# Cross-attention over 128-wide heads: the TensorE order of a two-head turn and its PSUM banks

## The chip, the core and the metric

The kernel runs on one core of a Trainium2 chip. A core has TensorE (matrix products into PSUM, 8 banks of 128x512 fp32), VectorE (DVE), ScalarE (ACT), GpSimd (POOL) and SyncE (SP, which here issues the DMAs). Each engine works through its own queue in order and waits on semaphores for the others. The metric is the device time of one execution in microseconds.

## The reference, cut to what matters

Four transformer blocks run one after the other on x (8, 128, 256). The change is in the third, which is two cross-attentions of 16 heads of width 128 against the same context (8, 128, 256):

```
for i in (1, 2):
    h = layer_norm(x, scale_i, offset_i)
    qh = (h @ wq + bq).reshape(b, 128, 16, 128)
    kh = (ctx @ wk + bk).reshape(b, 128, 16, 128)
    vh = (ctx @ wv + bv).reshape(b, 128, 16, 128)
    kh = concatenate([kh, bias_k]); vh = concatenate([vh, bias_v])   # one more key and value
    weights = softmax(einsum('bqhk,bthk->bhqt', qh, kh) / sqrt(128))
    x = x + einsum('bhqt,bthk->bqhk', weights, vh).reshape(b, 128, 2048) @ wo + bo
```

All is fp32. The kernel subtracts bias_k and bias_v from keys and values beforehand, so that the extra key is a score of zero and bias_v is added back to every head's output.

## The kernel before

It has three stages: stage A (the first two blocks), the two cross-attentions (`TURNS`), and stage C (an MLP and the fourth block). Stages A and C follow orders written out by hand in tables (`ORDER_ONE`, `ORDER_TWO`); the change does not touch them. `TURNS` is a loop over (j, turn): j = 1 or 2 is the attention, turn = 0 to 7 a pair of heads. Every engine has its own copy of this loop, and the order of the calls in each copy is the order of its queue. In a turn TensorE makes, for its two heads h = 0, 1:

- Q and K (`project_heads`, L830): a head's queries or keys for all 8 batches, two banks, 12 products of 128x512 each (every fp32 operand is cut into a high and a low part, and three of the four part products are made);
- V (`values_of`, L844): values of both heads for two batches, four calls of 12 products, a bank each;
- S (`scores_of`, L858): 16 matmuls, two banks; T (`turn_weights`, L867): 8 transposes of the softmax weights, two banks; W (`weigh_heads`, L878): weights times values, 16 matmuls, two banks;
- O (`output`, L890): the projection of the turn before, four calls of 12 products, a bank each.

`claim` makes the first write of a bank wait until the bank's last contents are drained. VectorE drains S (maximum L1195 and shift L1200; the bank is free after the shift), V (L1220), Q (L971) and O (L1239, into x), makes the sums and reciprocals (L1207, L1211) and the low part of the heads' outputs (`OT lo`, L1227). ScalarE makes the exponentials, drains K (L1343) and T (L1510, into `PT`), and makes the high part of the heads' outputs (L1343). GpSimd divides by the sum (L1742), cuts the weights of later heads into parts (L1701, L1703) and copies two bias columns per head into `bcol` and a pair per turn into `bvcol` (L1732, L1733, L1792), from which the drains read them. SyncE loads the weights.

Banks before: S of head 0 in banks 0, 1 and of head 1 in 2, 3; T of both heads in 4, 5; W in 6, 7 (head 0 of turn 0: 2, 3); Q and K by `BANKS`. In turn 0 three of the four V calls are made ahead in banks 2, 3, 4 (`AHEAD`), and the fourth (called V3 below) goes to bank 5. TensorE's order in an ordinary turn is S0, O, O, Q1, K1, O, O, S1, V, V, V, V, T0, Q0', W0, T1, K0', W1, where the digit is the head and ' marks the next turn. Turn 0 is Q1, S0, S1, V3, Q0', K0', T0, T1, W0, W1. In the last turn K0' is replaced by other work (in j = 1 the first keys of j = 2, in j = 2 keys and values of stage C).

## Time and profile before

| | |
|---|---|
| median of 3 runs | 1048.21 us (1047.02 to 1049.92) |
| profiled execution, span | 1047.5 us |
| median less the profiled span | 0.7 us |
| stage A | 0 to about 299 us |
| turns of j = 1 and j = 2 | about 299 to 798 us |
| stage C | from about 798 us |
| an ordinary turn | 31.37 us, TensorE busy throughout |
| TensorE / VectorE / ScalarE / GpSimd busy | 97% / 68% / 57% / 59% |

The trace is of one execution. Its times run from the start of the span. A row of the timeline gives an instruction's start and duration; TensorE's matmuls overlap, so that what a block of them costs is the distance from its start to the start of the next block. The chain of waits follows the work that ended last back through what released it.

### The profile page before, as it was taken

Reading aid. Unit: us, or ns where it says so; the run is one execution under the profiler, and the core shown is the slowest. Engines: PE = TensorE matmul, PEld = TensorE weight load, DVE = VectorE, ACT = ScalarE, POOL = GpSimd, SP = SyncE. Lnnn points to the kernel's source line nnn. Section 1 sums busy time; section 2 is a strip of 40 time slices with the busy share of each in tenths; the row PEclk is TensorE's granted clock in tenths of the full one; section 3 lists DMA queues with packets and bytes.
Section 4 is the critical chain, followed back from the end, with each engine's and each line's share of the span. In section 5 each row is a group of like instructions: output and inputs, shape, how many; then the busy total and the mean of one; then the engine's idle time right before and its main releaser. Section 6 shows DMA issues by size and latency. Waiting matters only on the chain.

```text
span 1047.5 us, 21298 instructions
## 1 busy us (share of the span) xinstructions
PE 1011.3 (97%) x8275; PEld 908.5 (87%) x8275; DVE 711.9 (68%) x1141; ACT 593.4 (57%) x1296; POOL 614.3 (59%) x617
## 2 busy tenths in 40 slices
PE   7899999999999999999999999999998999989998
PEld 6788888888888999999988999999998888777877
DVE  7997888998266565655567655656556287898760
ACT  5998888797533333222334323332225479999982
POOL 5895476655554443333376445655444388999961
PEclk9999999999999999999999999999999999999999
DMA  9200001000112221202130111101000000000000
GB/s 340 103 2 2 1 2 42 2 1 2 51 61 81 81 82 61 78 25 81 41 104 1 42 40 42 41 21 41 22 10 2 1 1 2 2 1 2 12 12 21
DMA packets 33788, 40.74 MB, mean 39 GB/s; under 512 B 2111, under 2 KB 31257, under 8 KB 32025
## 3 DMA queue, kind: packets, MB, share of 16 engines
q1 hardware_dynamic: 33689, 39.38, 11.3%
q8 instruction: 67, 1.10, 0.4%
q14 instruction: 32, 0.26, 0.1%
HBM read 38.32 MB, written 1.05 MB: 38 GB/s over the span
## 4 chain that ended last, share of the span: by engine, by line
PE 73%; POOL 11%; DVE 6%; issue 5%; ACT 5%; DMA 0%; SPq 0%; POOLq 0%; DVEq 0%; ACTq 0%
PE psum L830 13%; PE psum L715 9%; PE psum L727 9%; PE psum L890 7%; PE psum L844 7%; PE psum L753 5%; PE psum L878 5%; PE psum L858 4%; POOL C tile L1647 3%; PE psum L642 3%; PE psum L743 3%; PE psum L768 2%; PE psum L867 2%; POOL C tile L1653 2%; PE psum L780 1%
## 5 line engine op out<-in xcount | busy, mean ns | idle before, releaser
L1742 POOL TENSOR_TENSOR B tile<-B tile,B rec 128x1024 f32<-128x1024 f32 x32 | 60.7, 1897 | 192.0 <-DVE B rec L1211 192.0
L1653 POOL TENSOR_TENSOR A tile<-A tile,outer rec 128x1024 f32<-128x1024 f32 x48 | 91.0, 1906 | 57.8 <-DVE outer rec L1089 57.7
L1428 ACT ACTIVATE A tile<-A tile,outer min 128x128 f32<-128x128 f32 (+1 forms) x256 | 92.3, 449 | 2.6 <-DVE outer min L1082 2.5
L1343 ACT ACTIVATE B kT<-psum,B bcol 128x1024 f32<-128x1024 f32 x32 | 35.7, 1115 | 98.9 <-PE psum L830 98.9
L1239 DVE TENSOR_TENSOR x_all<-x_all,psum 128x512 f32<-128x512 f32 x64 | 42.6, 683 | 55.2 <-PE psum L890 55.0
L1428 ACT ACTIVATE C tile<-C tile,outer min 128x128 f32<-128x128 f32 x256 | 77.8, 398 | 0.5 <-DVE outer min L1082 0.4
L1499 ACT ACTIVATE B tile<-B max 128x8 f32<-128x8 f32 x32 | 6.9, 215 | 123.4 <-DVE B max L1195 123.4
L971 DVE TENSOR_SCALAR B qT<-psum,B bcol 128x1024 f32<-128x1024 f32 x32 | 41.1, 1283 | 48.8 <-PE psum L830 48.7
L844 PE MATMUL psum<-B v hi,cT hi 128*128 128x256 f32 x256 | 73.5, 287 | 0.3 <-ACT B kT L1343 0.3
L844 PE MATMUL psum<-B v hi,cT lo 128*128 128x256 f32 x256 | 71.9, 281 | 0.0
L844 PE MATMUL psum<-B v lo,cT hi 128*128 128x256 f32 x256 | 71.9, 281 | 0.0
L878 PEld LDWEIGHTS psum<-B PT,B v 128*128 128x128 f32 x512 | 61.4, 191 | 3.4 <-ACT B PT L1510 1.4
L1653 POOL TENSOR_TENSOR C tile<-C tile,outer rec 128x1024 f32<-128x1024 f32 x32 | 60.6, 1898 | 6.0 <-DVE outer rec L1089 6.0
L878 PE MATMUL psum<-B PT,B v 128*128 128x128 f32 x512 | 62.1, 275 | 1.0 <-ACT B PT L1510 1.0
L1075 DVE TENSOR_TENSOR A tile<-m,psum 128x1024 f32<-128x1024 f32 x48 | 56.5, 1215 | 9.2 <-PE psum L743 8.0
L858 PE MATMUL psum<-B kT,B qT 128*128 128x128 f32 x512 | 62.1, 275 | 0.0
L1394 ACT COPY A PT<-psum 128x512 f32<-128x512 f32 x96 | 51.4, 591 | 18.1 <-PE psum L753 10.9
L1087 DVE TENSOR_REDUCE outer sum<-A tile 128x4 f32<-128x1024 f32 (+1 forms) x48 | 58.0, 1207 | 4.9 <-ACT A tile L1428 4.9
L858 PEld LDWEIGHTS psum<-B kT,B qT 128*128 128x128 f32 x512 | 59.9, 192 | 0.2
L1227 DVE SCALAR_TENSOR_TENSOR B OT1 lo<-psum,B bvcol,B OT1 hi 128x512 fp32r<-128x512 f32 x32 | 24.0, 751 | 51.3 <-ACT B OT1 hi L1343 50.1
L727 PE MATMUL psum<-weights,C aT 128*128 128x256 f32 x256 | 57.2, 380 | 1.2 <-ACT C aT L1385 1.2
L727 PE MATMUL psum<-weights,A aT 128*128 128x256 f32 x256 | 57.8, 380 | 0.1
(294 smaller groups left out, 3470.6 us busy)
## 6 DMA issues: line engine op xcount, KB each, us to landing
weights<-in_weights_c SPq DMA_DIRECT2D x6, 1024.0 KB, 6.3
raw<-in_wq SPq DMA_DIRECT2D x32, 128.0 KB, 2.6
raw<-in_wk SPq DMA_DIRECT2D x32, 128.0 KB, 2.9
raw<-in_wv SPq DMA_DIRECT2D x16, 256.0 KB, 2.8
raw<-in_wo SPq DMA_DIRECT2D x16, 256.0 KB, 2.7
weights<-in_weights_a SPq DMA_DIRECT2D x1, 3072.0 KB, 21.9
weights<-in_weights_a SPq DMA_DIRECT2D x1, 2048.0 KB, 11.3
wide<-in_bias_v SPq DMA_DIRECT2D x2, 1024.0 KB, 9.5
```

The lines of the kernel that those rows point to most:

```text
L715: i = pe.matmul(bank(z)[:, n * T:(n + 1) * T], w[wp][:, c, n * P:(n + 1) * P], h[hp][:, c, :], start=(c, wp, hp) == (0, 0, 0), stop=c == C ...
L727: i = pe.matmul(bank(z)[:, 0:D], part.aT(k)[:, c, b * P:(b + 1) * P], w2[:, c, :], start=c == 0, stop=c == FC - 1)
L830: i = pe.matmul(bank(banks[n]), wt[wp][:, c, :], src[sp][:, c, n * BANK:(n + 1) * BANK], start=(c, wp, sp) == (0, 0, 0), stop=c == C - 1 a ...
L844: i = pe.matmul(bank(z)[:, k * 2 * HK:(k + 1) * 2 * HK], m.bcT[cp][:, c, (2 * n + k) * S:(2 * n + k + 1) * S], m.cut["v"][wp][:, c, :], st ...
L858: i = pe.matmul(bank(2 * h + b // 4)[:, (b % 4) * S:(b % 4 + 1) * S], m.qT[h][:, b * S:(b + 1) * S], m.kT[h][:, b * S:(b + 1) * S], start= ...
L878: i = pe.matmul(bank(z)[:, k * P:(k + 1) * P], m.vv[:, 4 * n + k, h * HK:(h + 1) * HK], m.bPT[:, h, n, k * P:(k + 1) * P], start=True, sto ...
L890: i = pe.matmul(bank(z)[:, k * D:(k + 1) * D], m.bOT[h][op][:, (2 * n + k) * S:(2 * n + k + 1) * S], m.cut["o"][wp][:, h, :], start=(h, op ...
L1075: dve.tensor_tensor(tile(u, ly.nk), mask.to_broadcast(shape), sc, ALU.subtract).then_inc(s["masked"].sem, s["masked"].mark((st, u)))
L1087: dve.tensor_reduce(part.sum[:, u % 4, 0:ly.per], tile(u, ly.nk), AX.X, ALU.add).then_inc(s["sum_made"].sem, s["sum_made"].mark((st, u)))
L1428: i = act.activation(of_head, of_head, ACT.Exp, bias=part.min[:, u % 4, h:h + 1], scale=-1.0)
L1653: pool.tensor_tensor(tile(u, ly.nk), tile(u, ly.nk), part.rec[:, u % 4, 0:ly.per].unsqueeze(2).to_broadcast([P, ly.per, ly.nk]), ALU.mult) ...
L1742: pool.tensor_tensor(tv, tv, m.brec[:, h, :].unsqueeze(2).to_broadcast([P, B, S]), ALU.mult).then_inc(s["normalised"].sem, s["normalised"] ...
```

## The change

The loops are regrouped and the banks are dealt out anew.

- TensorE's ordinary turn becomes seven groups: S0 S1, O O O O, K0' K1', V V V V, T0 T1, Q0' Q1', W0 W1. Both heads of the next turn are projected in this turn. Turn 0 becomes Q1, S0, S1, V3, K0', K1', Q0', Q1', T0, T1, W0, W1, and the last turn has no Q' and, for K', the same other work as before, after T1.
- Banks alternate: an even turn's first set is banks 0 to 3 and its other set 4 to 7, in an odd turn the reverse. S, K', T and W use the first set; O, V and Q' use the other, which is the first set of the next turn. Turns 0 and 7 have exceptions. In turn 0, K0' goes to banks 4 and 5, K1' to 6 and 7, Q0' and Q1' to 0 to 3; V3 stays in bank 5.
- The queues of VectorE, ScalarE, GpSimd and SyncE are put in an order that goes with it: VectorE takes both heads' maxima and shifts first, ScalarE drains both K' before both T, GpSimd cuts weights in pairs and divides both heads one after the other, and SyncE loads weights in pairs.
- `bcol` and `bvcol`, their copies on GpSimd and the waits on them are gone. Drains read the bias column of a head in the table of columns (`cols`).

Nothing else is computed and the number and shapes of the matmuls are the same. The diff, cut to its core:

```diff
-BANKS = {("q", 0): (0, 1), ("k", 0): (2, 3), ("q", 1): (6, 7), ("k", 1): (4, 5)}
-def banks_of(kind, head):
-    return BANKS["q", 1] if (kind, head) == ("k", 2) else BANKS[kind, head % 2]
+def first_set(turn):
+    return turn % 2 * 4
+def other_set(turn):
+    return 4 - first_set(turn)
+FIRST_BANKS = {(1, "q", 0): 0, (1, "k", 0): 2, (1, "q", 1): 6, (1, "k", 1): 4, (2, "q", 0): 0, (2, "k", 0): 4, (2, "q", 1): 6, (2, "k", 1): 4}
+def head_bank(j, kind, head):
+    if head < 2:
+        return FIRST_BANKS[j, kind, head]
+    before = head // 2 - 1
+    first_goes_keys = (kind == "k") == (before > 0)
+    return (first_set(before) if first_goes_keys else other_set(before)) + 2 * (head % 2)
+def scores_bank(turn, h):
+    return first_set(turn) + 2 * h
+def values_bank(turn, n):
+    if turn == 0:
+        return (*AHEAD, 5)[n]
+    return (first_set(turn) if turn == NP_ - 1 else other_set(turn)) + n
+def turned_bank(turn, h):
+    return (first_set(turn) if 0 < turn < NP_ - 1 else other_set(turn)) + 2 * h
-    return 6 if turn or h else 2
+    if turn == NP_ - 1:
+        return (6, 0)[h]
+    return first_set(turn) + 2 * h
+def outputs_bank(turn, n):
+    return (0 if turn == NP_ - 1 else other_set(turn + 1)) + n
...
-            claim(banks[n], "bq_drained" if kind == "q" else "bk_drained", event)
+            claim(z + n, "bq_drained" if kind == "q" else "bk_drained", event)
...
+        event, z = (j, turn, h), scores_bank(turn, h)
     def turn_weights(j, turn, h):
+        z = turned_bank(turn, h)
-            claim(4 + n, "weights_drained", (j, turn, h, n))
+            claim(z + n, "weights_drained", (j, turn, h, n))
...
         last = turn == NP_ - 1
         if turn == 0:
             project_heads(j, "q", 1)
-            scores_of(j, 0, 0)
-            scores_of(j, 0, 1)
-            values_of(j, 0, 3, 5)
-            project_heads(j, "q", 2)
-            project_heads(j, "k", 2)
-            turn_weights(j, 0, 0)
-            turn_weights(j, 0, 1)
-            weigh_heads(j, 0, 0)
-            weigh_heads(j, 0, 1)
+            for h in range(2):
+                scores_of(j, 0, h)
+            values_of(j, 0, 3)
+            project_pair(j, "k", 1)
+            project_pair(j, "q", 1)
+            for h in range(2):
+                turn_weights(j, 0, h)
+            for h in range(2):
+                weigh_heads(j, 0, h)
             continue
-        scores_of(j, turn, 0)
-        output(j, turn - 1, 0, 4)
-        output(j, turn - 1, 1, 5)
-        project_heads(j, "q", 2 * turn + 1)
-        project_heads(j, "k", 2 * turn + 1)
-        output(j, turn - 1, 2, 6)
-        output(j, turn - 1, 3, 7)
-        scores_of(j, turn, 1)
+        for h in range(2):
+            scores_of(j, turn, h)
         for n in range(4):
-            values_of(j, turn, n, 4 + n)
-        turn_weights(j, turn, 0)
+            output(j, turn - 1, n)
         if not last:
-            project_heads(j, "q", 2 * turn + 2)
+            project_pair(j, "k", turn + 1)
+        for n in range(4):
+            values_of(j, turn, n)
+        for h in range(2):
+            turn_weights(j, turn, h)
+        if not last:
+            project_pair(j, "q", turn + 1)
         elif j == 1:
             project_heads(2, "k", 0)
         else:
-            two("k", "L3c", 0, 0, 2)
-        weigh_heads(j, turn, 0)
-        turn_weights(j, turn, 1)
-        if not last:
-            project_heads(j, "k", 2 * turn + 2)
-        weigh_heads(j, turn, 1)
+            two("k", "L3c", 0, 0, 4)
+        for h in range(2):
+            weigh_heads(j, turn, h)
         if last and j == 1:
             project_heads(2, "k", 1, (0,))
             for n in range(4):
-                output(1, turn, n, n)
+                output(1, turn, n)
             project_heads(2, "k", 1, (1,))
             for n in range(NS):
                 pe.wait_ge(s["nxn_made"].sem, s["nxn_made"].at((n, SB - 1)))
                 features(("N", n), m.nxn[n], 6 + n % 2, "DVE" if n else "ACT")
                 if n != 2:
-                    values_ahead(2, min(n, 2))
+                    values_of(2, 0, min(n, 2))
             project_heads(2, "q", 0)
         elif last:
             two("v", "L3c", 0, 0, 5)
...
-        dve.wait_ge(s["bias_copied"].sem, s["bias_copied"].at((j, head)))
-        affine(m.qT[head % 2][:, :], m.psum[:, z:z + 2, :].rearrange("p a b -> p (a b)"), SCALEK, m.bcol[:, 1 - head % 2, 0:1]).then_inc(
+        affine(m.qT[head % 2][:, :], m.psum[:, z:z + 2, :].rearrange("p a b -> p (a b)"), SCALEK, m.col[f"L2_bq{j}"][:, head:head + 1]).then_inc(
...
         last = turn == NP_ - 1
         if turn == 0:
             queries_of(j, 1)
-            exponentials(j, 0, 0)
-            exponentials(j, 0, 1)
-            divide_by_sum(j, 0, 0)
-            divide_by_sum(j, 0, 1)
-            values_of(j, 0, 3)
-            queries_of(j, 2)
-            weigh_heads(j, 0, 0)
-            weigh_heads(j, 0, 1)
-            continue
-        exponentials(j, turn, 0)
-        output(j, turn - 1, 0, 4)
-        output(j, turn - 1, 1, 5)
-        queries_of(j, 2 * turn + 1)
-        output(j, turn - 1, 2, 6)
-        output(j, turn - 1, 3, 7)
+        for h in range(2):
+            exponentials(j, turn, h)
+        if turn:
+            output(j, turn - 1, 0)
+            output(j, turn - 1, 1)
         divide_by_sum(j, turn, 0)
-        exponentials(j, turn, 1)
-        for n in range(4):
+        if turn:
+            output(j, turn - 1, 2)
+            output(j, turn - 1, 3)
+        divide_by_sum(j, turn, 1)
+        for n in range(4) if turn else (3,):
             values_of(j, turn, n)
-        divide_by_sum(j, turn, 1)
         if not last:
             queries_of(j, 2 * turn + 2)
-        weigh_heads(j, turn, 0)
-        weigh_heads(j, turn, 1)
+            queries_of(j, 2 * turn + 3)
+        for h in range(2):
+            weigh_heads(j, turn, h)
         if (j, turn) == (2, 3):
             dve.wait_ge(s["masks_loaded"].sem, 32)
             for mask in (m.ms, m.mc):
...
     for j, turn in TURNS:
         last = turn == NP_ - 1
-        exponentials(j, turn, 0)
-        if turn:
-            keys_of(j, 2 * turn + 1)
-        exponentials(j, turn, 1)
-        turn_weights(j, turn, 0)
-        if turn == 0:
-            keys_of(j, 2)
-            turn_weights(j, turn, 1)
-        elif last and j == 1:
+        for h in range(2):
+            exponentials(j, turn, h)
+        if not last:
+            keys_of(j, 2 * turn + 2)
+            keys_of(j, 2 * turn + 3)
+        for h in range(2):
+            turn_weights(j, turn, h)
+        if last and j == 1:
             keys_of(2, 0)
         elif last:
             two("k", "L3c", 0, 0)
-        weigh_heads(j, turn, 0)
-        if turn:
-            turn_weights(j, turn, 1)
-        if turn and not last:
-            keys_of(j, 2 * turn + 2)
-        weigh_heads(j, turn, 1)
+        for h in range(2):
+            weigh_heads(j, turn, h)
         if last and j == 1:
             next_xn(0)
             next_xn(1)
...
     for j, turn in TURNS:
         last = turn == NP_ - 1
+        if turn == 0:
+            cut_pair(j, "k", 1)
+        if not last:
+            cut_pair(j, "q", turn + 1)
         if turn:
-            biases(j, 2 * turn + 1)
-            if not last:
-                biases(j, 2 * turn + 2)
-            cut_qk(j, 2 * turn + 1)
             cut_values(j, turn)
-        else:
-            biases(j, 2)
-            cut_qk(j, 2)
-        divide(j, turn, 0)
-        before = earlier((j, turn), TURNS)
-        if before:
-            pool.wait_ge(s["ot_lo"].sem, s["ot_lo"].at((*before, 1, 1)))
-        pool.tensor_copy(m.bvcol[:, :], m.col[f"L2_bias_v{j}"][:, 2 * turn:2 * turn + 2]).then_inc(
-            s["bias_v_copied"].sem, s["bias_v_copied"].mark((j, turn)))
-        if turn == 0:
-            divide(j, turn, 1)
-        elif not last:
-            cut_qk(j, 2 * turn + 2)
-        elif last and j == 1:
-            biases(2, 0)
-            cut_qk(2, 0)
+        for h in range(2):
+            divide(j, turn, h)
+        if turn < NP_ - 2:
+            cut_pair(j, "k", turn + 2)
+        elif (j, turn) == (1, NP_ - 2):
+            cut_pair(2, "k", 0)
         cut_output(j, turn)
+        if (j, turn) == (1, NP_ - 1):
+            cut_pair(2, "q", 0)
         if j == 2 and 1 <= turn < 5:
             cut_up("M2", turn - 1)
+            cut_up("L3c", turn - 1)
         if j == 2 and turn >= 5:
             cut_weights("L3s", "qkv"[turn - 5])
-        if last and j == 1:
-            biases(2, 1)
-            cut_qk(2, 1)
-        if turn:
-            divide(j, turn, 1)
...
-    for j in (1, 2):
-        for turn in range(1, NP_):
-            load_qk(j, 2 * turn + 1)
-            load_v(j, turn)
-            load_o(j, turn)
-            if turn < NP_ - 1:
-                load_qk(j, 2 * turn + 2)
-            if j == 1 and turn < NP_ - 1:
-                at = (turn - 1) * PIECE
-                sp.dma_start(m.weights[:, at:at + PIECE], ins["weights_c"][:, at:at + PIECE]).then_inc(s["w_c_loaded"].sem, s["w_c_loaded"].mark(turn, 16))
-        if j == 1:
-            load_qk(2, 0)
-            load_qk(2, 1)
+    for j, turn in TURNS:
+        last = turn == NP_ - 1
+        if turn < NP_ - 2:
+            load_pair(j, "k", turn + 2)
+        elif (j, turn) == (1, NP_ - 2):
+            load_pair(2, "k", 0)
+        if not last:
+            load_v(j, turn + 1)
+            load_o(j, turn + 1)
+        if turn < NP_ - 2:
+            load_pair(j, "q", turn + 2)
+        elif (j, turn) == (1, NP_ - 2):
+            load_pair(2, "q", 0)
+        if j == 1 and 0 < turn < NP_ - 1:
+            at = (turn - 1) * PIECE
+            sp.dma_start(m.weights[:, at:at + PIECE], ins["weights_c"][:, at:at + PIECE]).then_inc(s["w_c_loaded"].sem, s["w_c_loaded"].mark(turn, 16))
+        if (j, turn) == (1, NP_ - 1):
             load_v(2, 0)
+            load_pair(2, "k", 1)
+            load_pair(2, "q", 1)
             sp.wait_ge(s["bv_drained"].sem, s["bv_drained"].at((1, NP_ - 1, 3)))
```

Where the change moves work, three places. First TensorE in turn 0 of j = 1, from the last product of V3 on. Before:

```order
L844 MATMUL psum<-B v hi,cT lo 128x256
L830 MATMUL psum<-B hT hi,B q1 hi 128x512 [waits bshifted,wlo_made]
L830 MATMUL psum<-B hT lo,B q1 hi 128x512
L830 MATMUL psum<-B hT hi,B q1 lo 128x512
L830 MATMUL psum<-B hT hi,B q1 hi 128x512
L830 MATMUL psum<-B hT lo,B q1 hi 128x512
L830 MATMUL psum<-B hT hi,B q1 lo 128x512
L830 MATMUL psum<-B hT hi,B q1 hi 128x512 [waits bshifted]
```

and now:

```order
L885 MATMUL psum<-B v hi,cT lo 128x256
L867 MATMUL psum<-cT hi,B k1 hi 128x512 [waits bv_drained,wlo_made]
L867 MATMUL psum<-cT lo,B k1 hi 128x512
L867 MATMUL psum<-cT hi,B k1 lo 128x512
L867 MATMUL psum<-cT hi,B k1 hi 128x512
L867 MATMUL psum<-cT lo,B k1 hi 128x512
L867 MATMUL psum<-cT hi,B k1 lo 128x512
L867 MATMUL psum<-cT hi,B k1 hi 128x512 [waits bv_drained]
```

Behind V3 stood Q0', whose two halves waited for the shifts of S0; now K0' stands there, whose halves wait for drains of V (`bv_drained`), the second one for that of V3 itself.

Second, VectorE in the same turn, from the maxima of S0 to the drains of W. Before:

```order
L1195 TENSOR_REDUCE B max<-psum 128x8 [waits scored]
L1200 SCALAR_TENSOR_TENSOR B tile<-B max,psum 128x8x128 [waits max_made]
L1195 TENSOR_REDUCE B max<-psum 128x8 [waits scored]
L1200 SCALAR_TENSOR_TENSOR B tile<-B max,psum 128x8x128 [waits max_made]
L1207 TENSOR_REDUCE B sum<-B tile 128x8 [waits exp_made]
L1211 RECIPROCAL B rec<-B sum 128x8 [waits summed]
L1207 TENSOR_REDUCE B sum<-B tile 128x8 [waits exp_made]
L1211 RECIPROCAL B rec<-B sum 128x8 [waits summed]
L1220 TENSOR_TENSOR B v<-psum,B bv 128x512 [waits v_projected]
L971 TENSOR_SCALAR B qT<-psum,B bcol 128x1024 [waits bias_copied,q_projected]
```

and now:

```order
L1231 TENSOR_REDUCE B max<-psum 128x8 [waits scored]
L1236 SCALAR_TENSOR_TENSOR B tile<-B max,psum 128x8x128 [waits max_made]
L1231 TENSOR_REDUCE B max<-psum 128x8 [waits scored]
L1236 SCALAR_TENSOR_TENSOR B tile<-B max,psum 128x8x128 [waits max_made]
L1243 TENSOR_REDUCE B sum<-B tile 128x8 [waits exp_made]
L1247 RECIPROCAL B rec<-B sum 128x8 [waits summed]
L1243 TENSOR_REDUCE B sum<-B tile 128x8 [waits exp_made]
L1247 RECIPROCAL B rec<-B sum 128x8 [waits summed]
L1256 TENSOR_TENSOR B v<-psum,B bv 128x512 [waits v_projected]
L1007 TENSOR_SCALAR B qT<-psum,cols 128x1024 [waits q_projected] x2
```

Up to the drain of V3 (the ninth row) nothing moved; behind it stand two drains of queries instead of one.

Third, ScalarE in the last turn of j = 1, from the second head's exponentials on. Before:

```order
L1499 ACTIVATE B tile<-B max 128x8 [waits summed,max_made]
L1502 ACTIVATE B tile<-B tile 128x1032 [waits bshifted,own_made]
L1510 COPY B PT<-psum 128x512 [waits weighed,weights_turned] x2
L1343 ACTIVATE B kT<-psum,B bcol 128x1024 [waits bias_copied,k_projected]
L1343 ACTIVATE B OT0 hi<-psum,B bvcol 128x512 [waits bias_v_copied,weighed] x2
L1510 COPY B PT<-psum 128x512 [waits weighed,weights_turned] x2
L1343 ACTIVATE B OT1 hi<-psum,B bvcol 128x512 [waits bias_v_copied,weighed] x2
```

and now:

```order
L1527 ACTIVATE B tile<-B max 128x8 [waits summed,max_made]
L1530 ACTIVATE B tile<-B tile 128x1032 [waits bshifted,own_made]
L1538 COPY B PT<-psum 128x512 [waits weighed,weights_turned] x4
L1372 ACTIVATE B kT<-psum,cols 128x1024 [waits k_projected]
L1372 ACTIVATE B OT0 hi<-psum,cols 128x512 [waits weighed] x2
L1372 ACTIVATE B OT1 hi<-psum,cols 128x512 [waits weighed] x2
```

The drains of T1 moved from between those of W0 and W1 to ahead of the keys.

## Rows read from the trace of the kernel before

**Rows 1.** The page: busy time by engine, and granted clock by slices.

```profile
PE 1011.3 (97%) x8275; PEld 908.5 (87%) x8275; DVE 711.9 (68%) x1141; ACT 593.4 (57%) x1296; POOL 614.3 (59%) x617
...
PEclk9999999999999999999999999999999999999999
```

**Rows 2.** One ordinary turn as a window, its columns in the first line.

```profile
core 0: us, PE busy (x) PEld busy (x) DVE busy (x) ACT busy (x) POOL busy (x), PEclk, DMA share, GB/s
387.68:419.05 31.37, 31.37 (x226) 29.36 (x225) 18.16 (x22) 9.48 (x14) 12.48 (x20) 1.00 0.21 68
```

**Rows 3.** Chain of waits in that turn: start us, us, what.

```profile
387.68 2.93 PE psum L890 x24
390.61 5.51 PE psum L830 x24
396.12 2.87 PE psum L890 x24
...
400.78 5.66 PE psum L844 x48
406.44 0.87 PE psum L867 x8
...
410.08 1.78 PE psum L878 x16
...
417.26 1.79 PE psum L858 x16
```

**Rows 4.** Timeline, turn 0, j = 1: start us, us, engine, line, operation.

```profile
311.07 0.40 PE L830 MATMUL psum<-B hT hi,B q1 hi 128*128 128x512 f32 x1
...
311.71 1.22 DVE L1200 SCALAR_TENSOR_TENSOR B tile<-B max,psum 128x1024 f32<-128x1024 f32 x1
...
315.73 0.64 DVE L1220 TENSOR_TENSOR B v<-psum,B bv 128x512 f32<-128x512 f32 x1
...
316.54 1.90 POOL L1742 TENSOR_TENSOR B tile<-B tile,B rec 128x1024 f32<-128x1024 f32 x1
...
318.49 0.33 PE L867 MATMUL psum<-ident,B tile 128*128 128x128 f32 x1 [0.87 <-POOL B tile L1742]
```

**Rows 5.** Timeline, turn 0, j = 2: the same places.

```profile
567.76 0.39 PE L830 MATMUL psum<-B hT hi,B q1 hi 128*128 128x512 f32 x1
...
572.12 0.64 DVE L1220 TENSOR_TENSOR B v<-psum,B bv 128x512 f32<-128x512 f32 x1
...
574.89 0.33 PE L867 MATMUL psum<-ident,B tile 128*128 128x128 f32 x1 [0.58 <-POOL B tile L1742]
```

**Rows 6.** Timeline, turn 7, j = 1: first S and first O.

```profile
511.20 1.95 PE L858 MATMUL psum<-B kT,B qT 128*128 128x128 f32 x16
...
542.65 0.35 PE L890 MATMUL psum<-B o hi,B OT0 hi 128*128 128x256 f32 x1 [0.22 <-issue]
```

**Rows 7.** Timeline, turn 7, j = 2: first S, end of W1, O.

```profile
767.60 1.61 PE L858 MATMUL psum<-B kT,B qT 128*128 128x128 f32 x13
...
796.06 0.37 PE L699 MATMUL psum<-C kv hi,cT hi 128*128 128x256 f32 x1
...
797.91 0.36 PE L890 MATMUL psum<-B o hi,B OT0 hi 128*128 128x256 f32 x1 [0.18 <-issue]
```

**Rows 8.** Timeline, S0 to O in an ordinary turn.

```profile
418.02 0.75 DVE L1227 SCALAR_TENSOR_TENSOR B OT1 lo<-psum,B bvcol,B OT1 hi 128x512 fp32r<-128x512 f32 x1
...
418.85 0.19 PEld L890 LDWEIGHTS psum<-B o hi,B OT0 hi 128*128 128x128 f32 x1
```

**Rows 9.** Timeline, transposes and the first queries after them.

```profile
406.28 1.03 PE L867 MATMUL psum<-ident,B tile 128*128 128x128 f32 x8
407.07 0.47 PE L830 MATMUL psum<-B hT hi,B q1 hi 128*128 128x512 f32 x1
407.38 0.40 PE L830 MATMUL psum<-B hT lo,B q1 hi 128*128 128x512 f32 x1
```

**Rows 10.** Timeline, the longest idle stretch of TensorE.

```profile
10.38 0.66 PE L621 MATMUL psum<-ident,A xn 128*128 128x128 f32 x4 [2.62 <-DVE A xn L1040]
```

## What the change should do to the time

> **What bounds the kernel now.** I read the page first: TensorE is busy for 97% of the span and its granted clock is in the highest tenth of every slice [rows 1]. A kernel of this kind can only become shorter where TensorE stands still, so all the other engines matter by the waits that they put on it. The window of an ordinary turn says the same more sharply: 31.37 us, of which TensorE is busy 31.37, VectorE 18.16 and GpSimd 12.48 [rows 2]. The chain of waits in that turn never leaves TensorE [rows 3], and its pieces price the blocks: S 1.79, W 1.78, T 0.87, V 5.66 for four, Q or K 5.51 for two, O 2.93 for the first two calls of a turn and 2.87 for the other two. With two S, two W, two T and twice two of Q and K that makes 3.58 + 3.56 + 1.74 + 5.66 + 11.02 + 5.80 = 31.36, the turn. The same products are made after the change. So the twelve ordinary turns cannot bring much, and I looked for where TensorE waits in the irregular ones: turn 0 and turn 7 of each attention, on the timeline.
>
> **Ordinary turns.** The one wait left there is at the first O. VectorE ends the last `OT lo` at 418.02 + 0.75 = 418.77, and TensorE loads the first weights of O at 418.85 [rows 8]; the first two calls of O cost 0.06 more than the other two [rows 3]. O needs that `OT lo`. How long after the end of W1 it comes is seen in turn 7 of j = 2: the first product behind W1 starts at 796.06 and O, held by nothing else, at 797.91, 1.85 us later [rows 7]. Before, only S0 (1.79) lay between W1 and O; now S0 and S1 (3.58) do, which covers 1.85 with 1.73 to spare. There are 7 such places in each attention, 14 in all: 14 x 0.06 = **-0.8 us**.
>
> The new order adds waits too; I checked each against its cover, counted from the start of S0. In turn 0 of j = 1, where VectorE already takes both heads' maxima and shifts one after the other, S0 starts 3.58 + 1.42 (V3, a quarter of 5.66) before 311.07, at 306.07, and the second shift ends at 311.71 + 1.22 = 312.93, so 6.86 after it [rows 3, 4]. K0' and K1' reuse the banks of S, and start at 3.58 + 5.80 = 9.38: covered by 2.5. GpSimd's second division ends at 318.44, 12.37 after S0 [rows 4]; four drains of O come ahead of it on VectorE now, some 0.64 each by the nearest row, a drain of V of the same size, so 14.9. T0 starts at 9.38 + 5.51 + 5.66 = 20.55: covered by 5.6. The weight cuts and their loads are asked for a whole turn ahead, on a GpSimd with 18.9 us free in a turn [rows 2]. I put all of these, and the queues that SyncE and GpSimd are reordered in, at nothing. The bias copies were on GpSimd, off the chain [rows 3], and their removal is worth nothing either; reading a column of `cols` in place has the operands' shape unchanged. If a cover were gone, each turn would lose what it lacks.
>
> **Turn 0.** Here a wait is added. K0' now follows V3 and takes banks 4 and 5, and bank 5 holds V3. Its second half waits for the drain of V3, and VectorE's order up to that drain did not change: maxima, shifts, sums, reciprocals, then V3. In j = 1 the block behind V3 starts at 311.07; half of a K is 5.51 / 4 = 1.38, so the second half could start at 312.45. The drain ends at 315.73 + 0.64 = 316.37, and an engine that is released starts about 0.05 later (GpSimd ends at 316.54 + 1.90 = 318.44, T1 starts at 318.49) [rows 4]. So TensorE waits from 312.45 to 316.42: **+3.97**. Queued behind it are K1', Q0', Q1', T, W and all the rest; nothing of that can go ahead. What goes: before, T0 started at 311.07 + 5.51 = 316.58 and ended at 317.45, and T1 waited for GpSimd until 318.49, 1.04. Now T0 comes after 316.42 + 1.38 + 2.76 + 5.51 = 326.07, long after 318.44: **-1.04**. In j = 2 the same: 567.76 + 1.38 = 569.14; drain 572.12 + 0.64 = 572.76, restart 572.81: **+3.67**; and T1 had waited from 567.76 + 5.51 + 0.87 = 574.14 to 574.89: **-0.75** [rows 5]. Both turns together: 3.97 + 3.67 - 1.04 - 0.75 = **+5.85 us**. That the earlier K1' and Q1' are made in turn 0 and not in turn 1 moves 5.51 and adds none.
>
> **Turn 7.** Here waits go. In j = 1 S0 starts at 511.20 and O at 542.65, 31.45 later [rows 6]. Now, from S0: S 3.58, O 5.80, V 5.66, T 1.74, the first K of j = 2 2.76, W 3.56: 23.10. Then 1.85 until O; half a K of 1.38 lies inside that, as before. With the 5.51 that moved to turn 6 it is 30.46: **-1.0**. The waits that went are those of T1 and W1, which followed each other too closely. In j = 2 S0 to O took 797.91 - 767.60 = 30.31 [rows 7]; now the K in the middle is one of stage C, 12 products at 5.66 / 48 each, 1.42: 23.10 - 2.76 + 1.42 + 1.85 + 5.51 = 29.12: **-1.2**.
>
> **The sum.** 5.85 - 0.84 - 0.99 - 1.19 = **+2.8 us**. On the profiled span of 1047.5 that is 1050.3; the median of the runs is 0.7 above that span, so 1051.0, or +0.27%. About 0.3% (3.1 us) is what a measurement of this kernel can tell from no change, so the forecast lies just inside "no change".
>
> **Rivals.**
> A, the sum above: 1051.0. For it: the bank numbers and the order of VectorE's queue leave no way around the wait.
>
> B, slower by TensorE's clock. The new idle stretches, some 3.8 and 3.5 us once the tails of the running products are taken off, are longer than any in this trace: the longest is 2.62 us, at 10.38, and the clock stayed up around it [rows 1, 10]. No row here shows what a longer one does. If the clock is at 1.2 instead of 2.4 GHz for the rest of K0' and for K1', 1.38 + 2.76 = 4.14 us take twice as long: with one of the two stretches 1048.2 + 2.8 + 4.1 = 1055.1, with both 1059.3. It decides right behind the wait. Against it: the stretches are isolated, TensorE being fully busy on both sides. The Trainium skill ("TensorE: Matmul & The Clock Gate", section "HAM oscillation — how this bites in real kernels") warns that gaps in which TensorE idles make the clock fall and the next products start slow. By that rule B's price would be paid, in one stretch or both; that the clock stayed up around the gap of rows 10 neither confirms nor refutes it.
>
> C, slower by `OT lo`. In the ordinary turn VectorE now drains Q1' just ahead of the four `OT lo`. If that makes the last one later than 3.58 us after W1, O waits in all 14 places; it decides at a delay of 1.73. At a delay of 2.0 it costs 14 x 0.27 = 3.8 more: 1054.8. Against it: Q1' ends before W0 starts, so its drain falls into W's 3.56 us.
>
> D, faster: the wait of turn 0 does not come, because K0' finds bank 5 empty. Then 2.83 - 3.97 - 3.67 = -4.8: 1043.4. Against it: the order rows name the drain.
>
> E, switches. The first queries after transposes take 407.38 - 407.07 = 0.31 to the next, against 5.51 / 24 = 0.23 [rows 3, 9]. If 0.08 is lost at every change from whole fp32 matmuls to cut products, two of four such changes per turn go: 14 x 2 x 0.08 = 2.2, and the sum is +0.6: 1048.8. Against it: the transposes themselves start only 407.07 - 406.28 = 0.79 before, where the chain gives them 0.87 [rows 3, 9], so it is one and the same 0.08 seen twice.
>
> **How the numbers follow.** A 0.73, B 0.10, C 0.07, D 0.05, E 0.05. A's own uncertainty is the spread of medians (the three runs lie 2.9 us apart) and some tenths in each term: 1050.0 to 1052.2, of which about 0.23 lies over the bound of 1051.4 and 0.50 under it. Faster is D, 0.05; no change is 0.50 of A and E, 0.55; slower is 0.23 + 0.10 + 0.07 = 0.40. For 8 in 10 the range takes in A with its bounds, C, and B with one slow stretch, and leaves out D, most of E and B with two: 1049.0 to 1055.2.
>
> **What would show it.** Right: in the changed profile a wait of TensorE at the keys' line (L867 there) for VectorE's drain of V, near 4.0 and 3.7 us, once in each attention; no wait at the transposes in turn 0; ordinary turns of 31.30; the time from S0 to O in the last turns 24.9 and 23.6; granted clock 1.00 behind both waits. Wrong: a clock under 1.00 there (B), a wait for `OT lo` at O in ordinary turns (C), no wait at the keys (D), ordinary turns of 31.2 or less (E).

## The result: slower, 1.006 times the time before

The changed kernel takes 1054.78 us (median of 5 executions, 1052.37 to 1058.32), the kernel before 1049.23 on the same chip (5 executions, 1047.02 to 1049.92). The ratio is 1.006, with a 95% interval of 1.0044 to 1.0076. In the experiments' series the changed kernel was timed once more, beside another series of the kernel before: 1.0055 (1.0041 to 1.0069). So it is slower by 5 to 6 us. Forecast were 2.8, called no change; the measured time lies inside the range, but the change is clear of the noise, and about twice what the sum had.

The page of the changed kernel, its lines for busy time and granted clock, against [rows 1]:

```profile
PE 1012.2 (96%) x8275; PEld 910.5 (87%) x8275; DVE 709.6 (68%) x1141; ACT 594.9 (57%) x1296; POOL 605.8 (58%) x537
...
PEclk9999999999998999999999999999999999999999
```

The granted clock is the share of its full 2.4 GHz that TensorE was given; 0.5 is 1.2 GHz. Its mean in this execution, over a span of 1051.1 us, is 0.997, and the row of the clock has one 8, in the thirteenth slice, where turn 0 of j = 1 lies. GpSimd has 80 instructions fewer, the bias copies. The timeline of TensorE there, the halves of K0' (start us, us, engine, line, operation, idle before and its releaser), and the drain of V3 on VectorE:

```profile
310.94 0.39 PE L867 MATMUL psum<-cT hi,B k1 lo 128*128 128x512 f32 x1
315.12 0.79 PE L867 MATMUL psum<-cT hi,B k1 hi 128*128 128x512 f32 x1 [3.79 <-DVE B v L1256]
315.71 0.63 PE L867 MATMUL psum<-cT lo,B k1 hi 128*128 128x512 f32 x1
316.14 0.63 PE L867 MATMUL psum<-cT hi,B k1 lo 128*128 128x512 f32 x1
...
320.83 0.43 PE L867 MATMUL psum<-cT lo,B k0 hi 128*128 128x512 f32 x1
321.10 0.39 PE L867 MATMUL psum<-cT hi,B k0 lo 128*128 128x512 f32 x1
321.33 0.39 PE L867 MATMUL psum<-cT hi,B k0 hi 128*128 128x512 f32 x1
```

```profile
314.43 0.64 DVE L1256 TENSOR_TENSOR B v<-psum,B bv 128x512 f32<-128x512 f32 x1
```

Two things are to be seen. The wait: the next product would have started at 310.94 + 0.23 = 311.17 and starts at 315.12, when the drain has ended (314.43 + 0.64 = 315.07). And behind it the products start 0.43 us apart instead of 0.23, until 320.83. The same stretch in windows, wait, slow products, the rest of the block up to T0, and below it the same place of j = 2 (columns as in [rows 2]; the granted clock is the third number from the end):

```profile
311.16:315.12 3.96, 0.17 (x1) 0.00 (x1) 3.76 (x6) 1.69 (x3) 1.86 (x2) 0.87 0.00 0
315.12:321.04 5.92, 5.92 (x14) 4.67 (x15) 0.00 (x0) 1.11 (x1) 3.02 (x4) 0.51 0.00 0
321.04:327.49 6.45, 6.45 (x29) 5.24 (x29) 1.28 (x1) 1.12 (x1) 2.97 (x4) 1.00 0.15 37
571.68:575.34 3.66, 0.17 (x1) 0.00 (x0) 3.54 (x6) 1.06 (x1) 1.86 (x2) 1.00 0.00 0
575.34:579.00 3.66, 3.66 (x16) 3.04 (x17) 0.00 (x0) 1.12 (x1) 2.98 (x4) 1.00 0.00 0
```

The clock was at 1.2 GHz from about 1 us before the end of the wait (0.87 over 3.96 us) and through the slow products (0.51 over 5.92 us). The first interval is 0.36 us too long and the twelve after it 0.2 each: 2.8 us. In j = 2 TensorE stood still nearly as long, 3.66 us, and kept 2.4 GHz in this execution.

An ordinary turn, against [rows 2], and TensorE's waits in the turns, before and after (line, waited for: us in total, times, longest):

```profile
387.00:418.29 31.29, 31.29 (x225) 29.31 (x224) 18.18 (x22) 9.61 (x15) 11.92 (x14) 1.00 0.21 68
```

```profile
PE psum L867 <- POOL B tile L1742: 1.8, 3, 0.9
PE psum L830 <- DVE B hT lo L1161: 1.2, 1, 1.2
PE psum L878 <- ACT B PT L1510: 1.0, 2, 0.7
```

```profile
PE psum L867 <- DVE B v L1256: 7.3, 2, 3.8
PE psum L867 <- DVE B hT lo L1197: 1.3, 1, 1.3
```

The waits of transposes for GpSimd and of W for ScalarE are gone; 7.3 us for the drain of V3 are new.

**Where the time went.** I take the stretch from the first product of Q1 of j = 1 to the first O behind turn 7 of j = 2: 301.88 to 797.91 before, 300.62 to 801.59 after, 496.03 and 500.97 us. Stage C has the same length in both; stage A ended 1.3 us earlier in the profiled execution of after, whose first inputs had come sooner. The stretch is +4.94: +2.8 of slow products, and +2.1 of order and waits, where the prediction's sum had +2.8 in all. The medians lie 5.6 and 5.3 us apart in the two series; less the 2.1, 3.2 to 3.5 are left for the clock, over and above what falls of the clock cost the kernel before.

### The profile page after: what moved, and what is told of

It reads as the page before. It is cut to its first block, busy times and chain, and to the rows that moved or that the text cites. A ratio compares the mean times of both kernels' runs of the same rounds, so it can differ in the third digit from the quotient of the medians.

```text
span 1051.1 us, 21061 instructions
## 1 busy us (share of the span) xinstructions
PE 1012.2 (96%) x8275; PEld 910.5 (87%) x8275; DVE 709.6 (68%) x1141; ACT 594.9 (57%) x1296; POOL 605.8 (58%) x537
## 4 chain that ended last, share of the span: by engine, by line
PE 79%; POOL 8%; DVE 6%; ACT 4%; issue 1%; DMA 0%; SPq 0%; DVEq 0%; ACTq 0%; POOLq 0%
PE psum L867 16%; PE psum L752 9%; PE psum L764 9%; PE psum L930 8%; PE psum L885 8%; PE psum L917 5%; PE psum L896 5%; PE psum L790 5%; POOL C tile L1669 3%; PE psum L679 3%; PE psum L906 3%; PE psum L780 3%; PE psum L805 2%; POOL C tile L1675 2%; PE psum L817 1%
## 5 line engine op out<-in xcount | busy, mean ns | idle before, releaser
L1007 DVE TENSOR_SCALAR B qT<-psum,cols 128x1024 f32<-128x1024 f32 (+1 forms) x38 | 44.0, 1166 | 87.7 <-PE psum L867 86.3
L1256 DVE TENSOR_TENSOR B v<-psum,B bv 128x512 f32<-128x512 f32 x64 | 43.5, 687 | 81.6 <-PE psum L885 81.6
L1372 ACT ACTIVATE B kT<-psum,cols 128x1024 f32<-128x1024 f32 x32 | 35.7, 1115 | 93.4 <-PE psum L867 93.4
L1538 ACT COPY B PT<-psum 128x512 f32<-128x512 f32 x64 | 32.9, 601 | 84.0 <-PE psum L906 84.0
L1372 ACT ACTIVATE B OT0 hi<-psum,cols 128x512 fp32r<-128x512 f32 x32 | 21.9, 688 | 70.9 <-PE psum L917 70.8
L896 PE MATMUL psum<-B kT,B qT 128*128 128x128 f32 x512 | 59.9, 276 | 0.0
L917 PE MATMUL psum<-B PT,B v 128*128 128x128 f32 x512 | 59.7, 275 | 0.0
```

Source lines behind the costliest of these rows:

```text
L896: i = pe.matmul(bank(z + b // 4)[:, (b % 4) * S:(b % 4 + 1) * S], m.qT[h][:, b * S:(b + 1) * S], m.kT[h][:, b * S:(b + 1) * S], start=True ...
L917: i = pe.matmul(bank(z)[:, k * P:(k + 1) * P], m.vv[:, 4 * n + k, h * HK:(h + 1) * HK], m.bPT[:, h, n, k * P:(k + 1) * P], start=True, sto ...
L1372: return act.activation(dst, src, ACT.Identity, bias=0.0 if bias is None else bias, scale=1.0 if scale is None else scale)
```

## The theories, and what tells them apart

**Theory 1**: the order is worth what the sum says, the waits of turn 0 cost their length and, besides, bring TensorE's clock down behind them, behind one or both of them. At two waits that is several us per execution. **Rivals**: the low clock is the chip's or the day's and not the order's; only the longer wait does it; or some part of the new order other than the waits makes the kernel slow.

For the clock, one profile of one execution is not enough, so I use the mean granted clock of every execution. At a span of 1050 us a mean of 0.998 stands for some 4 us at 1.2 GHz, 0.997 for 6, 0.995 for 10. A mean doesn't say where in the kernel the clock was low; only the profiled execution of each run does. For the rest I use the stretch above, in which a shift of stage A has no part. x1 to x4 ran on one chip, x5 to x8a on a second, x9 to x11 on a third, each beside the kernel before. All experiments, with the two waits of TensorE between the halves of K0' (of Q0' in the last row), from start to start less the usual distance of two matmuls:

| kernel | long waits, us | stretch, us | median, us | ratio (95%) | executions by mean clock: 1.00 / 0.998 / 0.997 / lower |
|---|---|---|---|---|---|
| before, three series | none | 496.03 | 1047.94, 1048.64, 1049.20 | 1 | 34 / 21 / 7 / 1 |
| after, both series | 3.96, 3.66 | 500.97, 501.56 | 1054.78, 1053.98 | 1.0060, 1.0055 | 0 / 0 / 3 / 8 |
| x1, x11: queries first | none | 491.69 | 1043.67, 1043.33 | 0.9955 (0.9942 to 0.9969), 0.9944 (0.9930 to 0.9958) | 8 / 3 / 0 / 0 |
| x2: second key first | 1.16, 0.89 | 492.83 | 1044.83 | 0.9966 (0.9953 to 0.9979) | 4 / 1 / 0 / 0 |
| x4: drain earlier | 1.12, 1.03 | 492.87 | 1044.64 | 0.9969 (0.9959 to 0.9979) | 7 / 2 / 3 / 0 |
| x3: waits filled | 0.55, 0.28 left | 498.46 | 1050.65 | 1.0022 (1.0014 to 1.0031) | 7 / 4 / 0 / 0 |
| x7: waits half filled | 2.29, 2.06 left | 500.02 | 1053.23 | 1.0050 (1.0033 to 1.0067) | 0 / 2 / 2 / 2 |
| x5: wait in j = 1 only | 3.96 | 496.46 | 1049.33 | 1.0009 (0.9999 to 1.0019) | 0 / 3 / 5 / 4 |
| x6: wait in j = 2 only | 3.75 | 497.54 | 1048.72 | 1.0000 (0.9991 to 1.0008) | 0 / 6 / 6 / 0 |
| x9: biases in place, old order | none | 495.47 | 1047.67 | 0.9989 (0.9978 to 1.0000) | 6 / 6 / 0 / 0 |
| x10: waits in the old order | 3.96, 3.71 | 506.21 | 1059.93 | 1.0101 (1.0084 to 1.0118) | 0 / 0 / 0 / 4 |

## Experiments that take the wait away

**x1, queries before keys in turn 0.** Q0' and Q1' go to banks 0 to 3, which are free by then; K0' comes 5.5 us later, when V3 has been drained.

```diff
             values_of(j, 0, 3)
-            project_pair(j, "k", 1)
             project_pair(j, "q", 1)
+            project_pair(j, "k", 1)
```

> The changed kernel with one edit: in turn 0 of each attention TensorE makes the two Q' ahead of the two K', so the K' that shares bank 5 with V3 comes 5.5 us later. Theory 1 (the loss is the wait for V3's drain, 3.96 and 3.66 us in the profile, and the fall of TensorE's clock that the idle stretch brings, on average some 3 us more): both waits are gone, the granted clock is 1.00 throughout, and the time falls from 1054.8 by 7.6 + about 3 to 1044, ratio to the kernel before 0.995 to 0.997. Theory 2 (the clock falls for the new order of blocks as such, or the loss lies in the ordinary turns): the time stays above 1049 or the clock below 1.00 in some runs.

Measured: 1043.67 us, ratio 0.9955, 1.0% under the changed kernel. The stretch is 9.28 us shorter than in the changed kernel. The window of turn 0 from 311 to 322 shows TensorE busy throughout:

```profile
311.00:322.00 11.00, 11.00 (x53) 9.10 (x52) 6.85 (x8) 4.01 (x6) 5.30 (x5) 1.00 0.01 1
```

In place of the waits a short one has come at T1, for ScalarE, which drains the two keys ahead of the transposes:

```profile
322.75 0.96 PE L906 MATMUL psum<-ident,B tile 128*128 128x128 f32 x7 [0.42 <-ACT B kT L1372]
```

By start-to-start times it costs 0.59 in each attention. So 3.96 + 3.66 - 2 x 0.59 = 6.44 of the 9.28 are waits; the other 2.84 are the slow products of that execution, as counted above. Two of the six executions had a mean clock of 0.998 where 1.00 throughout was expected; of the kernel before on this chip 8 of 23 were below 1.00. The rest of the new order, alone at last, is worth 491.69 - 496.03 = -4.34 us against the kernel before.

**x11, the same kernel again**, beside x9 and x10.

> The changed kernel with queries first in turn 0 once more, beside the two others on one chip, for a verdict on the best version and for how often the clock falls where no long wait stands in turn 0. Earlier: 1043.67, ratio 0.9955. Expected: 0.995 to 0.997, with mean clock 1.00 in half of the executions or more and 0.998 in the others; the idle stretches left are those that the kernel before has too. A clock under 1.00 in every execution would speak against the waits of turn 0 as the cause.

Measured: 1043.33, ratio 0.9944, four of five executions at clock 1.00. It is the fastest version here, ahead of both kernels.

**x2, second key first.** K1' has its own banks 6 and 7; K0' with the half that waits comes behind it.

```diff
-            project_pair(j, "k", 1)
+            project_heads(j, "k", 3)
+            project_heads(j, "k", 2)
```

> The changed kernel with one edit: in turn 0 the K' of head 1 (banks 6, 7) is made before the K' of head 0 (banks 4, 5), which moves the contested half by 2.75 us. Theory 1: the wait shrinks from 3.96 to 1.2 us and from 3.66 to 0.9 us, the stretch is shorter than the 2.6 us around which the clock stayed up in the kernel before, so the clock stays 1.00 in every run; 1054.8 - 5.5 - about 3 = 1046, ratio 0.997 to 0.999. If the clock falls for any idleness at all, the ratio is 1.000 to 1.003 and the clock column below 1.00.

Measured: 1044.83, ratio 0.9966, somewhat better than the 1046 and 0.997 to 0.999 expected, with one execution of five at 0.998. K1' covers its 2.8 us of the wait, and 1.16 and 0.89 are left:

```profile
316.29 0.50 PE L867 MATMUL psum<-cT hi,B k1 hi 128*128 128x512 f32 x1 [0.99 <-DVE B v L1257]
```

**x4, the drain earlier.** TensorE's order is that of the changed kernel; VectorE drains V3 before the two sums instead of behind them.

```diff
         if turn:
             output(j, turn - 1, 0)
             output(j, turn - 1, 1)
+        if turn == 0:
+            values_of(j, turn, 3)
         divide_by_sum(j, turn, 0)
...
-        for n in range(4) if turn else (3,):
+        for n in range(4) if turn else ():
             values_of(j, turn, n)
```

> The changed kernel with one edit on VectorE: in turn 0 the drain of V3 stands before the two sums and reciprocals, TensorE's order untouched. Theory 1 (VectorE's position of that drain is the cause of the wait): the drain ends some 2.9 us earlier, the wait is about 1.0 us, the sums come 0.65 us later and T0 still finds its weights divided; clock 1.00; time 1046, ratio 0.996 to 0.999. A rival, that TensorE is held by something else at that place (the cut weights of K', the bank's other half): the wait stays 3.7 to 4.0 us and the time 1054.

Measured: 1044.64, where 1046 was expected. Clock 1.00 was expected too, and 5 of 12 executions were below it. On VectorE the drain now stands straight behind the second shift, and TensorE waits 1.12 and 1.03:

```profile
310.16 1.22 DVE L1236 SCALAR_TENSOR_TENSOR B tile<-B max,psum 128x1024 f32<-128x1024 f32 x1
311.30 0.68 DVE L1256 TENSOR_TENSOR B v<-psum,B bv 128x512 f32<-128x512 f32 x1
```

Three edits on two engines, which share only that the wait is short or gone, all bring the kernel to 1044 to 1045. The wait behind V3 is the cause, with what hangs on it; the rest of the regrouping is not slow.

## Experiments that part the wait from the clock

**x3, the wait filled.** TensorE waits as long, but is kept at work: 32 transposes of the identity, which nothing reads, stand between the halves of K0'. They write to bank 6, so TensorE first waits until the queries that lay there are drained.

```diff
-            project_pair(j, "k", 1)
+            project_heads(j, "k", 2, (0,))
+            pe.wait_ge(s["bq_drained"].sem, s["bq_drained"].at((j, "q", 1)))
+            for _ in range(32):
+                pe.transpose(bank(6)[:, 0:P], m.ident[:, :], m.ident[:, :])
+            project_heads(j, "k", 2, (1,))
+            project_heads(j, "k", 3)
```

> The changed kernel, where TensorE makes 32 transposes of the identity (3.5 us of work whose result nobody reads) between the first half of K0' and the half that waits for V3's drain. The wait itself is not shortened. Theory 1 with the clock as its own term: the clock is 1.00 in every run and the time is the changed kernel's less the clock's part alone, 1054.8 - 3 to 5 = 1050 to 1051.5, ratio 1.001 to 1.002. If the clock were no cause, the time stays at 1054.8.

```profile
310.79 3.65 PE L960 MATMUL psum<-ident 128*128 128x128 f32 x32
314.83 0.47 PE L867 MATMUL psum<-cT hi,B k1 hi 128*128 128x512 f32 x1 [0.39 <-DVE B v L1261]
```

Measured: 1050.65, where the changed kernel takes 1054 to 1055. The path is no shorter (the second half still starts when the drain has ended; its stretch is 6.77 above that of x1, the 6.44 and 0.33 more), only the idling is gone, and with it some 4 us (by the ratios, which leave the chips out, 1.0055 or 1.0060 less 1.0022: 3.5 to 4.0). Seven of eleven executions have clock 1.00, in the changed kernel none. The other four are at 0.998, which was not expected, but so are 7 of 23 of the kernel before on this chip. That prices the two parts apart: the waits 6.4 us, the clock about 4.

**x8a, the changed kernel again.**

> The changed kernel as it is, beside the next three on one chip, for the spread of its granted clock. With both waits of turn 0 (3.96 and 3.66 us) and the clock at 1.00 it would take what the kernel with queries first takes plus 3.96 + 3.66 - 2 x 0.59 = 6.4, so 1050.1 us. Theory 1 (the clock falls behind the waits, not always behind both): most executions have a mean clock of 0.993 to 0.997, and the median is 1053 to 1056. Rival (the low clock belonged to the first chip, not to the order of the work): mean clock 1.00 in most executions, as in the four kernels without the idle stretches, and a median near 1050.5.

Measured: 1053.98, no execution above 0.997; the lowest, 0.992, took 1055.85 and 1056.3. In this profiled execution the clock fell behind both waits; the slow products cost 1.7 us behind each:

```profile
315.03:319.50 4.47, 4.47 (x13) 3.50 (x14) 0.00 (x0) 1.11 (x1) 3.02 (x4) 0.62 0.00 0
...
574.19:579.00 4.81, 4.81 (x14) 3.81 (x15) 0.00 (x0) 1.11 (x1) 3.02 (x4) 0.65 0.00 0
```

In both series none of the changed kernel's executions was without a fall, while 11 of 23 executions of the kernel before, on the chip of x8a, were: the chip is not the cause.

**x5 and x6, one wait each.** Queries first in one attention, keys first in the other (x6 has `j == 2`).

```diff
-            project_pair(j, "k", 1)
-            project_pair(j, "q", 1)
+            for kind in ("kq" if j == 1 else "qk"):
+                project_pair(j, kind, 1)
```

> Keys first in turn 0 of j = 1 as in the changed kernel, queries first in turn 0 of j = 2, so that one of the two waits is left. At full clock: 1043.67 (queries first in both) + 3.96 - 0.59 = 1047.0. Theory 1: the clock falls behind this one wait in most executions and costs some 3.0 us more there, so mean clocks of 0.997 and times near 1050; none of 0.995 or lower unless the clock falls elsewhere too. If the clock only falls when there are two such waits: 1047.0 at clock 1.00.

> The mirror image: queries first in j = 1, keys first in j = 2. At full clock 1043.67 + 3.66 - 0.59 = 1046.7. In the profiled execution of the changed kernel the clock stayed at 1.00 behind this wait and fell behind the other. Theory 1 (both stretches can bring the clock down, each with its own luck): some executions at 1.00 and 1046.7, others at 0.997 and 1049.7. Theory 1b (only the longer stretch, that of j = 1, does): 1046.7 at 1.00 throughout, as often as with queries first in both.

The windows of TensorE in x5 (end of the wait, behind it, further on), then in x6:

```profile
311.00:315.28 4.28, 0.49 (x4) 0.06 (x2) 4.08 (x6) 2.00 (x3) 1.86 (x2) 0.94 0.00 0
315.28:318.20 2.92, 2.92 (x7) 2.34 (x8) 0.00 (x0) 0.00 (x0) 1.89 (x2) 0.51 0.00 0
318.20:322.00 3.80, 3.80 (x19) 3.07 (x18) 0.00 (x0) 2.09 (x2) 2.00 (x4) 1.00 0.00 0
```

```profile
566.00:569.40 3.40, 0.00 (x0) 0.00 (x0) 3.28 (x6) 1.06 (x1) 1.86 (x2) 0.83 0.00 0
569.40:575.30 5.90, 5.90 (x14) 4.66 (x15) 0.00 (x0) 1.11 (x1) 3.03 (x4) 0.52 0.00 0
575.30:579.00 3.70, 3.70 (x17) 3.01 (x17) 0.00 (x0) 1.12 (x1) 2.34 (x4) 1.00 0.00 0
```

Measured: 1049.33 and 1048.72. No execution of either, 24 in all, kept clock 1.00. So one wait is enough, and that of j = 2, which had kept its clock in the changed kernel's first profile, brings it down too: theory 1b, only the longer one, falls. Theory 1 had expected some executions of x6 at 1.00, and there were none. Four of x5 were at 0.995, more than one fall of the profiled kind gives; where their clock was low is not known. How deep differs by execution. The profiled one of x5 lost 1.4 us, that of x6 2.7, by the stretch less the waits: 496.46 - 491.69 - (3.96 - 0.59) and 497.54 - 491.69 - (3.75 - 0.59). My number of 3.0 for each fall was the upper end; the executions at 0.998 took about 1048.0 in x5 and 1047.5 in x6, about 1 above the 1047.0 and 1046.7 that the expectations work out for full clock.

**x7, half filled.** As x3, with `range(16)`.

> The changed kernel with 16 transposes of the identity (nothing reads them) between the two halves of K0' in turn 0, in place of the 32 of the earlier run: 16 x 0.109 = 1.7 us of each wait are worked through, 2.2 and 1.9 us stay idle. The waits end when the drain ends in any case, so at full clock the time is 1050.1 to 1050.6. Theory 1 with the length of the stretch deciding: clock 1.00 in most executions, since the idle stretches are now no longer than the 2.62 us that stand in the trace of the kernel before without a fall: 1050.6. If every wait at this place brings the clock down, whatever its length: mean clocks of 0.993 to 0.997 as in the changed kernel, 1053 to 1056.

Measured: 1053.23, and no execution at 1.00. The expectation was wrong: with 2.3 and 2.1 us left of the waits the clock still falls. No run parts the length of the stand from what lies ahead of it, here transposes and not products. In the profiled execution the clock held behind the longer stand and fell behind the shorter, here as first products at 0.23 us from each other and then at 0.4:

```profile
575.43 0.47 PE L867 MATMUL psum<-cT hi,B k1 hi 128*128 128x512 f32 x1 [1.90 <-DVE B v L1261]
575.75 0.39 PE L867 MATMUL psum<-cT lo,B k1 hi 128*128 128x512 f32 x1
...
576.82 0.63 PE L867 MATMUL psum<-cT hi,B k1 lo 128*128 128x512 f32 x1
577.25 0.63 PE L867 MATMUL psum<-cT hi,B k0 hi 128*128 128x512 f32 x1
```

That execution had falls in two further places: around the wait at 10 us of [rows 10], here 2.37 us long, and behind two short waits for ScalarE near 1015 us, at the end of stage C (windows, columns as before). The kernel before has both places, so its own falls may lie there; its one profiled execution shows none at either.

```profile
10.00:14.00 4.00, 4.00 (x19) 3.93 (x20) 2.18 (x8) 1.50 (x3) 0.00 (x0) 0.59 1.06 382
...
1017.00:1021.00 4.00, 4.00 (x38) 3.62 (x31) 0.42 (x1) 2.20 (x6) 2.12 (x2) 0.60 0.00 0
```

**x10, the wait in the old order.** The kernel before with one line added, so that TensorE waits for the drain of V3 between the halves of Q0'.

```diff
-            project_heads(j, "q", 2)
+            project_heads(j, "q", 2, (0,))
+            pe.wait_ge(s["bv_drained"].sem, s["bv_drained"].at((j, 0, 3)))
+            project_heads(j, "q", 2, (1,))
             project_heads(j, "k", 2)
```

> The kernel before, with one wait added and nothing else: in turn 0 of both attentions TensorE waits for the drain of V3 between the two halves of Q0', the block that stands behind V3 there, where the changed kernel waits between the halves of K0'. By the terms of the prediction the wait is +3.97 and +3.67, and T1's own waits of 1.04 and 0.75 go: +5.85 us at full clock, 1053.5 to 1053.8. Theory 1 (an idle stretch of this length at this place brings the clock down, whatever the order around it): no execution at clock 1.00, most of 0.995 to 0.997, and 1.5 to 3 us more behind each wait, so 1056 to 1060. Rival (the clock falls because of the new order, for instance because whole fp32 products of keys run into projections): clock 1.00 in half of the executions, as in the kernel before, and 1053.6.

Measured: 1059.93, ratio 1.0101, all four executions at 0.995 or lower. Its windows at the end of the first wait and behind it:

```profile
314.00:317.83 3.83, 0.03 (x1) 0.00 (x0) 3.63 (x6) 1.56 (x3) 1.85 (x2) 0.98 0.00 0
317.83:321.10 3.27, 3.27 (x8) 2.59 (x9) 0.30 (x1) 0.00 (x0) 3.19 (x5) 0.50 0.00 0
```

The waits are 3.96 and 3.71, and T1 keeps 0.49 of its own in each attention, now for ScalarE, so they add 7.67 - (1.04 - 0.49) - (0.74 - 0.49) = 6.9, not 5.85. The stretch is 10.18 longer, which leaves 3.3 for the clock, 1.6 and 1.7 behind the two waits. (This execution, too, had a fall around 10 us, outside the stretch.) Neither the wait nor the fall needs the new order: the rival that the order makes the clock fall is out.

**x9, biases in place alone.** The kernel before without `bcol`, `bvcol`, their copies and waits; one of the three drains as an example:

```diff
-        dve.wait_ge(s["bias_copied"].sem, s["bias_copied"].at((j, head)))
-        affine(m.qT[head % 2][:, :], m.psum[:, z:z + 2, :].rearrange("p a b -> p (a b)"), SCALEK, m.bcol[:, 1 - head % 2, 0:1]).then_inc(
+        affine(m.qT[head % 2][:, :], m.psum[:, z:z + 2, :].rearrange("p a b -> p (a b)"), SCALEK, m.col[f"L2_bq{j}"][:, head:head + 1]).then_inc(
```

> The kernel before, with its order and its banks, and only the bias columns read in place: the copies into bcol and bvcol on GpSimd and the waits on them are gone. The prediction put this part at nothing, since the copies stand off the chain. Expected: ratio 1.000, within 0.1%, clock as in the kernel before. If the copies had held a drain back somewhere (the ordinary turn, or T1 in turn 0, which waits for GpSimd's division with bias copies ahead of it): up to 1.8 us faster, the 1.04 + 0.75 of T1.

Measured: 0.9989, an interval that ends at 1.0000; the stretch is 0.56 shorter. Part is to be seen: the copy of `bvcol` stood between GpSimd's two divisions, and T1's waits of turn 0 go from 1.04 to 0.91 and from 0.74 to 0.66. In turn 7 of j = 1 T1's wait of 0.50 is gone and W1's is 0.54 instead of 0.40, 0.4 less together. An ordinary turn still takes 31.37. By the trace it is not nothing, then, but about half a us; the times alone, with their interval up to 1.0000, hardly show it.

## Why the prediction was wrong: point by point

**The wait of turn 0: right.** Forecast 3.97 and 3.67, at K0' for V3's drain; measured 3.96 and 3.66. T1's waits of 1.04 and 0.75 went, as forecast.

**Ordinary turns: right.** Forecast 31.30, measured 31.29 in each of the twelve; the wait for `OT lo` at O is gone. TensorE's chain in that turn, against [rows 3]:

```profile
395.55 3.57 PE psum L896 x32
399.12 5.75 PE psum L930 x48
404.87 5.51 PE psum L867 x24
```

Four calls of O take 5.75, where they took 5.80. Rival C, a late `OT lo`, is out; E, gains at changes of operation, would need 31.2 or less, and is out; D, no wait, too.

**Turn 7: right, a little low.** S0 to O took 24.62 in j = 1 (forecast 24.9) and 23.51 in j = 2 (23.6):

```profile
545.15 0.36 PE L930 MATMUL psum<-B o hi,B OT0 hi 128*128 128x256 f32 x1 [0.22 <-issue]
```

```profile
801.59 0.36 PE L930 MATMUL psum<-B o hi,B OT0 hi 128*128 128x256 f32 x1 [0.42 <-issue]
```

The gains are 1.3 and 1.3 instead of 1.0 and 1.2.

**The bias copies: nearly right.** Put at nothing, worth some 0.5 us in the old order (x9), all of it in waits of T1 and W1 that the new order takes away by itself.

**The sum: right for what it held.** It gave +2.8 at full clock. Measured at full clock it is 491.69 + 6.44 - 496.03 = +2.1. The 0.7 between them are some 0.3 in turn 7 with its O, 0.2 in the twelve ordinary turns (shorter by 0.08 each and not by 0.06), and the rest in turn 0.

**The clock: the step that failed.** The sum put the clock behind the two new waits at nothing. The ground was "Against it: the stretches are isolated, TensorE being fully busy on both sides", which gave rival B a chance of 0.10. It was no rival but a term of the sum, worth about 4 us: in 11 executions of the changed kernel, 24 with one wait and 4 of x10, none stayed at clock 1.00, while half of those of the kernel before did. Isolation was no protection. The ground for the other belief was thin, too: the one long wait of the kernel before, [rows 10], had kept its clock in one profiled execution, and x7 shows the clock at 0.59 behind a wait of 2.37 us at the same place. One execution can't show that a wait is harmless when the clock falls in some executions and not in others; the spread of 2.9 us among three runs of one kernel was a hint of that. The passage of the Trainium skill that the prediction weighed ("TensorE: Matmul & The Clock Gate", section "HAM oscillation — how this bites in real kernels") says that such gaps bring the clock down, and the runs agree with it: no execution with such a wait stayed at 1.00.

B had the mechanism but not the price. It charged 4.1 us for each slow stretch; traced falls cost 1.4 (x5) to 2.8 (x6 and the first wait of the changed kernel), and x3 against the changed kernel gives about 4 for both waits together. So it is luck that B with one slow stretch, 1055.1, nearly meets the 1054.78 measured: two waits at about half its price each come to nearly the same. By B's own terms two slow stretches would have given 1059.3. The range, too, reached beyond 1052.2 only for the sake of B and C.

What stays open: which of two equal waits brings the clock down in a given execution and for how long, and how short a wait must be to be safe. Waits of 0.9 to 1.2 us (x2, x4) left 11 of 17 executions at 1.00, much like the kernel before; but 3 of 12 of x4 were at 0.997, against 1 of 23 there, too few to tell whether its waits of 1.1 us take a part. Waits of 2.1 to 2.3 us left none of six. Between them nothing was tried.

## What to carry to other kernels

When a regrouping puts a wait on an engine that is otherwise always busy, price the wait twice: its length, and TensorE's clock behind it. Then look at what the wait is for: here another order of two independent blocks, or a drain moved past two reductions, made a change that lost 0.6% into one that gains 0.5% or 0.3%. And where executions of one kernel differ from each other, here by 2.9 us in three, look at the mean clock of each of them before reading anything from a single profile.

## What the runs showed of the hardware

- With a single wait of 3.7 to 4.0 us of TensorE between fully busy stretches no execution of 24 kept a mean clock of 1.00 (x5, x6), with two of 2.1 to 2.3 us none of 6 (x7). Not each wait brings a fall: behind 3.66 us the clock stayed at 1.00 in one profiled execution of the changed kernel and fell in the other.
- The low level, 1.2 GHz, lasted some 3 us (x5) to 7 us (the changed kernel, x6). Products of 128x512 then started 0.43 us apart instead of 0.23.
- The fall began before the wait ended in some cases (0.87 over the wait of the changed kernel, 0.83 over its last 3.4 us in x6) and about 1 us after the restart in others (x7, 576.4 against 575.4).
- Useless transposes kept the clock up: 32 of them in each wait brought some 4 us back (x3); 16 did not keep it up (x7).
